# Two transformer layers on one core: an order of work of its own for the first and last windows of each layer, and an earlier load of the second causal window

## The chip, the cores and the metric

One core of one Trainium2 chip runs the whole program in one launch. The metric is the time of one execution on the device in microseconds; the number compared is the median of several executions. A change below 0.2% of it is not told apart from none here.

## The reference, cut to what matters

The input `x` is (4, 1024, 128) in float32. Four residual steps follow one another, each on the layer norm of `x`:

```python
x = x + attn_a(layernorm(x))     # 16 heads of 8, softmax over all 1024 keys
x = x + ffn(layernorm(x))        # silu(x Wg^T) * (x Wu^T), then Wd^T; hidden 384
x = x + attn_b(layernorm(x))     # the same attention with a causal mask
x = x + ffn(layernorm(x))
```

In the attention `q, k, v` come from one projection with bias, the scores are divided by sqrt(8), and an output projection with bias follows.

## The kernel before

Layer 0 is the attention over all keys, layer 1 the causal one. Each has 16 windows: 4 sequences by 4 groups of 4 heads (named a to d here). A window has two halves of 512 queries (f = 0, 1). Its work is of five kinds:

- A **job** (L1110, TensorE) computes 128 queries by up to 512 keys of plain scores into one PSUM bank, and VectorE takes their row maxima (L888, or L884 with the mask on the diagonal). Layer 0 has 64 jobs for a window, layer 1 has 36. Jobs go round a ring of banks: 3 to 6 in layer 0, 4 to 6 in layer 1.
- A **shift** unit: when the jobs of a half are done, GpSimd splits the negated maxima in two parts, TensorE transposes them (L1162), ScalarE copies them to `shift_rows` (L672), and SyncE sends them by DMA into two rows of the query operand (L433). The scores of that half wait for the DMA.
- A **scores** unit (L1144, in layer 1 with mask products L1152): 128 keys by 512 queries with the shift, for one head (single) or two (double-width), into one or two banks; ScalarE takes the exponential out of PSUM into `probs` (L656). A step is the four heads of one key block. Layer 0 uses single units in a ring of banks 0 to 2, and in its last window from step 5 on double-width units in banks 0-1 and 2-3. Layer 1 uses double-width units in the same two pairs throughout.
- The **sums** of a step (L1178): the four heads' probabilities by the values, into bank 7; after a half ScalarE copies the bank out (L663).
- A **norm** unit: TensorE transposes those sums (L1036), ScalarE copies them to `att_raw` (L677), VectorE inverts the denominators (L919), GpSimd multiplies (L549).

Every engine walks the same list, `Plan.walk`, in order. It is written out by hand as one string of letters for a window: j a job, s a scores unit, p sums, h and H the shift of half 0 and 1, N and n the norm of half 0 and 1. In the kernel before, that one string is repeated for all windows, with jobs some 48 (layer 0) or 37 (layer 1) ahead of the scores; at the ends of a layer letters that fall outside are dropped. A scores, shift or norm unit may start on TensorE when the unit that last had its banks has been copied out (`units_before`); the first double-width unit of layer 0 waits for all units before it and for all jobs.

While the last window's scores are still running, each layer starts on chunk 0 of the output projection and the feed-forward (`early_chunk`, at the steps `project_at`): ScalarE gathers heads (L686), TensorE transposes (L1036), ScalarE copies (`copy_ot`, L693), TensorE projects (`project`, L1194, bank 6), VectorE adds and normalises, TensorE transposes (`transpose_ffn_xn`), ScalarE copies (`copy_ffn_xt`, L700) and VectorE takes the remainder (`split_ffn_xt`, L943); then the same gather and transposes for chunk 1. Banks 4 and 5 hold these transposes.

Between the layers the feed-forward of layer 0 and the projections of layer 1 run chunk by chunk. SyncE stores each chunk's query and key parts to DRAM (`store_parts`, after L628 on ScalarE and L816 on VectorE) and loads a window's operands from there (`load_operands`, 14 DMAs, 1 MB); three operand buffers go round. Window 0 of layer 1 is loaded after the second chunk is stored, window 1 only after the last. Both belong to sequence 0, that is to the first two chunks. Some 18 (TensorE) or 22 (VectorE) jobs of layer 1 already run in this stage.

Of the kernel before, what the change touches and what calls it, by code (L numbers as in the profile page):

```python
# [14 lines left out]
B, S, E, H = 4, 1024, 128, 16  # L15
# [16 lines left out]
WINDOWS = B * GROUPS  # L32
# [12 lines left out]
BUFS = 3  # L45
PROBS = 6
PROB_STEPS = PROBS // 2
SEM_DMA = 16


class Plan:
# [9 lines left out]

    def __init__(self, causal, heads, unit_ring, job_ring, alternate, order, jobs_ahead, sums_behind, project_at, wide_step=99, tiles=None):
# [4 lines left out]
        self.paired = range(0 if causal else jobs_ahead)  # L69
# [9 lines left out]
        stream = []  # L79
# [20 lines left out]
        ends = {"H": ("shift", 0, 1), "h": ("shift", 1, 0), "N": ("norm", 0, 0), "n": ("norm", -1, 1)}  # L100

        self.walk = []
        jobs = taken = 0
        last_unit = {}
        for turn in range(-2, WINDOWS + 1):
            j, u, k = jobs_ahead, 0, -sums_behind
            for letter in order:
                if letter == "j":
                    w, x = turn + j // len(stream), stream[j % len(stream)]
                    j += 1  # L110
                    if 0 <= w < WINDOWS:
                        self.walk.append(("job", w, jobs, x))
                        jobs += 1
                elif letter == "s":
                    w, x = turn, units[u]
                    u += 1
                    if w == WINDOWS - 1 and x[0] >= wide_step:
                        if x[1][0] % 2 == 1:
                            continue
                        x = x[0], (x[1][0], x[1][0] + 1)  # L120
                        self.wide_from = min(self.wide_from, taken)
                    if 0 <= w < WINDOWS:
                        self.walk.append(("scores", w, taken, x))
                        last_unit[w, x[0]] = taken
                        taken += 1
                elif letter == "p":
                    w, x = turn + k // n, k % n
                    k += 1
                    if 0 <= w < WINDOWS:
                        self.walk.append(("sums", w, last_unit[w, x], x))  # L130
                else:
                    kind, dw, f = ends[letter]
                    if 0 <= turn + dw < WINDOWS:
                        self.walk.append((kind, turn + dw, taken, f))
                        taken += 1
        assert all(item[0] != "job" for item in self.walk[[i for i, item in enumerate(self.walk) if item[0] == "scores"
                                                           and item[2] >= self.wide_from][0]:]) if wide_step < n else True
# [12 lines left out]

    def ends_half(self, job):
# [2 lines left out]

PAIR_UNITS, HEAD_UNITS = ((0, 1), (2, 3)), ((0,), (1,), (2,), (3,))
PLANS = [Plan(causal=False, heads=HEAD_UNITS, unit_ring=3, job_ring=4, alternate=True,
              order="sjjsjpsjjjsspsjjsjspsjjsjspsjsjsjjsjssjjsjspHssjjsjpsjjsjspjjsjsspjsjssjsjjsnjsjjsspjssjsjpjssjsjpjssjsjpsjjsjspsjjsjspsjjsjsjsjsjsNhjjsjsspssjjjsps",
              jobs_ahead=48, sums_behind=2, project_at=(9, 11, 14), wide_step=5),
         Plan(causal=True, heads=PAIR_UNITS, unit_ring=2, job_ring=3, alternate=True,
              order="jsjjsjHpjssjjsspjjjssppjsjsjpjjssjpjjsjspjjsjspjjsjspjjjhnNjsjjspjjsjspjjssp",  # L160
              jobs_ahead=37, sums_behind=1, project_at=(4, 6, 10),
              tiles=("230 130 330 000+020 200+220 110+310 010+210 300+320 030 100+120",
                     "231 200 101+121 031 220 301+321 000 310 201+221 331 110 001+021 300 230 131 010 130 030 120 320 011+211 100 020 111+311 210 330"))]
# [7 lines left out]
def transformer_pair_kernel(nc, x_in, wqkv_a, bqkv_a, wout_a, bout_a, wqkv_b, bqkv_b, wout_b, bout_b,  # L171
# [10 lines left out]
    with ExitStack() as ctx:  # L182
# [171 lines left out]
        def _(sp):  # L354
# [46 lines left out]
            for layer, plan in enumerate(PLANS):  # L401
# [183 lines left out]
        def _(act):  # L585
# [56 lines left out]
            for layer, plan in enumerate(PLANS):  # L642
# [59 lines left out]
                def early_chunk(i):  # L702

                    if i == plan.project_at[0] - 1:
                        act.wait_ge(att_ready, half_base + 2 * GROUPS + 2)
                        gather_heads(0, 0)
                    if i == plan.project_at[0]:
                        copy_ot(0, 4)
                    if i == plan.project_at[2]:
                        copy_ffn_xt(0, 4)  # L710
                        gather_heads(1, 1)
                        copy_ot(1, 5)

                def take_weights(k):
                    act.wait_ge(setup_psum, 2 + k)
# [57 lines left out]
        def _(dve):  # L773
# [140 lines left out]
            for layer, plan in enumerate(PLANS):  # L914
# [30 lines left out]
                def early_chunk(i):  # L945

                    if i == plan.project_at[1]:
                        dve.wait_ge(x_biased, layer + 1)
                        add_projection(0)
                        projected_moments(0)  # L950
                        normalise_rows(0)
                    if i == plan.project_at[2]:
                        split_ffn_xt(0, 4)
# [59 lines left out]
        def _(pe):  # L1013
# [105 lines left out]
            for layer, plan in enumerate(PLANS):  # L1119
# [81 lines left out]
                def early_chunk(i):  # L1201

                    if i == plan.project_at[0]:
                        pe.wait_ge(ring_free, job_base + plan.jobs_all)
                        transpose_ot(0, 4)
# [123 lines left out]
```

## Time and profile before

| | |
|---|---|
| Median of 3 runs | 1323.11 us (1322.62 to 1324.69) |
| The profiled execution | 1321.39 us, of which its span 1319.5 us |
| Busy: TensorE, VectorE, ScalarE | 96%, 88%, 76% of the span |
| Layer 0's last job to its last exponential | 670.45 to 705.22 us |
| Layer 1's window 0, first scores to the next window's first | 832.40 to 863.42 us |

Times in the views count from the start of the span. PE is TensorE, DVE VectorE, ACT ScalarE, POOL GpSimd, SP SyncE. A row of a timeline gives start, length, engine, line, operation, what it writes and reads, how many in a row, and in brackets the engine's idle time before it and what ended it. In a row of a stretch each engine has its busy time and the number of its instructions; then come the granted clock of TensorE (1.00 is 2.4 GHz, 0.50 is 1.2 GHz), the busy share of the DMA engines and GB/s.

### The profile page before, as it was taken

The page shows a single profiled execution, that of the slowest core. Times are in us where ns is not written, and L with a number is a line of the kernel's source. Part 1 is how long each engine was busy: PE and PEld are TensorE (multiplying, and loading weights), DVE is VectorE, ACT ScalarE, POOL GpSimd, SP SyncE. Part 2 cuts the span into 40 slices and gives each one's busy share as a digit, 9 for nine tenths or more (in the row PEclk, how much of TensorE's full clock was granted, in tenths as well). Part 3 has the DMA queues.
Part 4 walks back from the last instruction along what each step waited for, and adds up shares of the span by engine and source line. Part 5 has one row for each costly group of instructions (what it writes and reads, how often), then busy time and mean ns, then how long its engine had stood idle before and what let it go on. Part 6 is the DMA issues. An engine that isn't in the chain of part 4 may idle for free.

```text
span 1319.5 us, 26665 instructions
## 1 busy us (share of the span) xinstructions
PE 1270.7 (96%) x9681; PEld 648.6 (49%) x9681; DVE 1162.8 (88%) x2979; ACT 1002.3 (76%) x1791; POOL 142.6 (11%) x309
## 2 busy tenths in 40 slices
PE   8899999999999999999997998899999999999898
PEld 6444343434343434343434875455555555555487
DVE  7689999999999999999934988699999999999376
ACT  8678888888888888888885552477877777777743
POOL 5630000000000000000001210200000000000011
PEclk9689999999999999999998997699999999999999
DMA  7611011111011111001000242212211221130001
GB/s 212 206 33 34 16 20 34 34 34 34 18 17 34 34 33 34 22 14 34 2 2 0 81 128 86 60 35 51 51 35 34 55 47 35 37 64 2 3 25 40
DMA packets 40059, 58.43 MB, mean 44 GB/s; under 512 B 7796, under 2 KB 19448, under 8 KB 39928
## 3 DMA queue, kind: packets, MB, share of 16 engines
q1 hardware_dynamic: 39928, 56.72, 18.0%
q8 instruction: 77, 1.26, 0.4%
q14 instruction: 54, 0.44, 0.1%
HBM read 36.77 MB, written 18.87 MB: 42 GB/s over the span
## 4 chain that ended last, share of the span: by engine, by line
PE 88%; DVE 5%; ACT 3%; issue 2%; DMA 1%; POOL 1%; SPq 0%; DVEq 0%; POOLq 0%
PE psum L1178 30%; PE psum L1110 21%; PE psum L1144 20%; PE psum L1265 4%; PE psum L1036 3%; PE psum L1249 2%; PE psum L1152 2%; ACT probs L656 2%; DVE maxima L888 1%; PE psum L1047 1%; DVE hid L966 1%; PE psum L1194 1%; PE psum L1085 1%; PE psum L1021 1%; PE psum L1162 1%
## 5 line engine op out<-in xcount | busy, mean ns | idle before, releaser
L656 ACT ACTIVATE probs<-psum 128x512 f32<-128x512 f32 (+3 forms) x1386 | 822.1, 669 | 174.2 <-PE psum L1144 89.5
L888 DVE TENSOR_REDUCE maxima<-psum 128x1 f32<-128x512 f32 x1232 | 767.8, 680 | 27.0 <-PE psum L1110 23.9
L1144 PE MATMUL psum<-qop,kop 64*128 64x512 f32 (+3 forms) x1792 | 513.7, 422 | 9.1 <-ACT probs L656 7.5
L1110 PE MATMUL psum<-kop,qop 62*128 62x512 f32 (+2 forms) x1744 | 499.7, 426 | 9.8 <-DMA kop<-k_parts 5.5
L1178 PE MATMUL psum<-probs,v 128*32 128x512 f32 (+3 forms) x3584 | 436.6, 563 | 1.1 <-ACT sums L663 1.1
L1144 PEld LDWEIGHTS psum<-qop,kop 64*128 64x128 f32 x1792 | 255.4, 188 | 213.4 <-ACT probs L656 186.2
L1110 PEld LDWEIGHTS psum<-kop,qop 62*128 62x128 f32 x1744 | 252.4, 189 | 214.8 <-DVE maxima L884 93.7
L884 DVE CUSTOM_DVE_ANT_0 junk<-psum,mask 128x384 bf16<-128x384 f32 (+3 forms) x512 | 222.3, 485 | 20.5 <-PE psum L1110 20.1
L1178 PEld LDWEIGHTS psum<-probs,v 128*32 128x32 f32 x3584 | 72.4, 109 | 112.8 <-issue 83.4
L1152 PE MATMUL psum<-half_ident,key_mask 64*128 64x64 bf16 x1024 | 83.2, 197 | 0.0
L539 POOL TENSOR_TENSOR shift<-negmax,zeros 128x16 bf16<-128x16 f32 x64 | 14.1, 220 | 567.6 <-DVE negmax L896 557.4
L549 POOL TENSOR_TENSOR att<-att_raw,rden 128x128 f32<-128x128 f32 x64 | 26.1, 407 | 423.8 <-DVE rden L919 423.8
L1249 PE MATMUL psum<-ffn_xt,gate_up_w 128*128 128x512 f32 x192 | 52.6, 409 | 6.0 <-DVE hid L966 5.9
L796 DVE TENSOR_TENSOR x<-psum,x 128x512 f32<-128x512 f32 x32 | 22.1, 689 | 38.6 <-PE psum L1194 24.9
L1152 PEld LDWEIGHTS psum<-half_ident,key_mask 64*128 64x128 bf16 x1024 | 45.3, 96 | 19.7 <-issue 8.2
L1265 PE MATMUL psum<-down_w,hid 128*128 128x128 f32 x384 | 49.0, 285 | 4.7 <-DVE hid L966 4.7
L748 ACT ACTIVATE hid<-psum 128x512 f32<-128x512 f32 x48 | 28.4, 597 | 30.3 <-PE psum L1249 30.0
L1265 PEld LDWEIGHTS psum<-down_w,hid 128*128 128x128 f32 x384 | 46.1, 198 | 7.8 <-DVE hid L966 7.2
L623 ACT ACTIVATE qk<-psum,bqk 128x512 f32<-128x512 f32 x32 | 21.1, 682 | 36.2 <-PE psum L1047 36.1
L884 DVE DVE_READ_ACCUMULATOR2_ANT maxima<- 128x1 f32 x512 | 42.4, 83 | 0.0
L1036 PE MATMUL psum<-ident,sums 128*128 128x128 f32 x256 | 38.7, 283 | 2.3 <-ACT sums L663 1.6
L1249 PEld LDWEIGHTS psum<-ffn_xt,gate_up_w 128*128 128x128 f32 x192 | 33.7, 189 | 14.7 <-DVE hid L966 8.4
(102 smaller groups left out, 732.2 us busy)
## 6 DMA issues: line engine op xcount, KB each, us to landing
qop<-q_parts SPq DMA_DIRECT2D x256, 64.0 KB
kop<-k_parts SPq DMA_DIRECT2D x64, 128.0 KB
kop<-k_parts SPq DMA_DIRECT2D x128, 64.0 KB
q_parts<-parts SPq DMA_DIRECT2D x24, 256.0 KB, 2.9
k_parts<-parts SPq DMA_DIRECT2D x24, 256.0 KB, 3.0
x<-in_L_attn_a_x SPq DMA_DIRECT2D x8, 256.0 KB, 4.2
q_parts<-att SPq DMA_DIRECT2D x8, 256.0 KB, 3.6
k_parts<-att SPq DMA_DIRECT2D x8, 256.0 KB, 3.8
```

The source lines that it names most:

```text
L549: nc.gpsimd.tensor_tensor(dst, att_raw[:, f, :, :, 0:HD], rden[:, f].rearrange("p t (h o) -> p t h o", o=1).broadcast_to([P, TPC, HG, HD]) ...
L656: nc.scalar.activation(probs[:, slot, heads[0] % 2:heads[-1] % 2 + 1, c0:], psum[:, bank:bank + len(heads), c0:], ACT.Exp, scale=SCORE_SCA ...
L748: nc.scalar.activation(hid[:, c, :], psum[:, 2 + 2 * (c % 2), :], ACT.Silu, scale=DEQUANT).then_inc(silu_ready, 1)
L884: ins = nc.vector.tensor_tensor_reduce(out=junk[:, slot, column:column + width], in0=src, in1=mask[:, CHUNK - width:], scale=1.0, scalar=L ...
L888: ins = nc.vector.tensor_reduce(dst, src, AX_X, ALU.max)
L1036: ins = nc.tensor.transpose(psum[:, bank, t * P:(t + 1) * P], src[:, t, :], ident[:])
L1110: ins = mm(psum[:, bank, column:column + width], qop[rows, buf, f, r, qb * P:(qb + 1) * P].bitcast(F32R), kop[rows, buf, r, kh * CHUNK:kh ...
L1144: ins = mm(psum[:, bank + k, c0:], kop[rows, buf, c // 2, j * P:(j + 1) * P].bitcast(F32R), qop[rows, buf, f, c // 2, c0:].bitcast(F32R), ...
L1152: ins = mm(psum[:, bank + k, at:at + TILE_ROWS], key_mask[rows, part, :], half_ident[rows], start=False, stop=part == 1)
L1178: ins = mm(psum[32 * c:32 * c + 32, 7, c0:], v[:, at:at + 32], probs[:, slot, c % 2, c0:], start=(j == 0), stop=(s == plan.half_end[f]), t ...
L1249: ins = mm(psum[:, 2 + 2 * (c % 2) + k, :], gate_up_w[:, k, c, :].bitcast(F32R), ffn_xt[:, part].bitcast(F32R), start=part == 0, stop=part ...
L1265: ins = mm(psum[:, 7, t * P:(t + 1) * P], hid[:, c, t * P:(t + 1) * P], down_w[:, c, :], start=(c == 0), stop=(c == FB - 1))
```

## The change

Each layer gets three strings: `opening` and `closing` are walked once, `order` (unchanged) 14 times between them. In layer 0 the opening gives the same list as before. In its closing, half 1's shift comes behind step 5 in place of three heads into step 4, double-width units begin at step 4 in place of 5, they go round three pairs of banks (0 to 5) in place of two, and the norms of window 14's half 1 and window 15's half 0 stand behind the last scores. As banks 4 and 5 are taken, `early_chunk` uses bank 6 for all transposes of layer 0, and TensorE waits for VectorE's `split_ffn_xt` ahead of the second `transpose_ot`. In layer 1 the opening has 32 jobs ahead of the first scores in place of 38, shift 0 stands behind 26 jobs in place of 29, the jobs of window 1 are spread among the scores, and the opening meets the old list at its place 110; in the closing shift 1 of the last window comes behind one more scores unit, norm 1 of window 14 comes earlier (ahead of step 4) and norm 0 of window 15 at the very end. SyncE loads window 1 of layer 1 straight behind window 0.

```diff
+WIDE_RING = 3
...
+        for letter in opening + order * (WINDOWS - 2) + closing:
...
     def bank(self, unit):
         if unit >= self.wide_from:
-            return (unit - self.wide_from) % 2 * 2
+            return (unit - self.wide_from) % WIDE_RING * 2
...
         if unit >= self.wide_from:
-            return unit - (unit > self.wide_from)
+            return unit - min(unit - self.wide_from, WIDE_RING - 1)
...
(layer 0)
+              closing="ssjpsjjsjspjsjjsspjjssjspsjjssjjssjjSSpSSpHSSpSSpSSpSpSSSpSpSSpSSpSSpSSpSnppNn",
-              jobs_ahead=48, sums_behind=2, project_at=(9, 11, 14), wide_step=5),
+              jobs_paired=48, project_at=(9, 11, 14)),
(layer 1)
+              opening="jjjjjjjjjjjjjjjjjjjjjjjjjjhjjjjjjsjjsjsjsjjpjjHsjsjspjjspjssjjpjsjsjpjsjjNhjssjjpjjssjjpjsjjpjjsjsjpjjsjspjjsjsjjsp",
               order="jsjjsjHpjssjjsspjjjssppjsjsjpjjssjpjjsjspjjsjspjjsjspjjjhnNjsjjspjjsjspjjssp",
-              jobs_ahead=37, sums_behind=1, project_at=(4, 6, 10),
+              closing="ssspHssspsspnssppsspsspsspsspsspsspssppNn",
+              jobs_paired=0, project_at=(4, 6, 10),
...
+CHUNK_BANKS = (6, 6, 6, 6), (4, 6, 4, 5)
...
                 load_operands(0, 0)
+                if layer == 1:
+                    load_operands(1, 1)
                 store_parts(layer, 1, 1)
...
                     sp.wait_ge(query_rows, 2)
-                load_operands(1, 1)
+                    load_operands(1, 1)
...
-                        copy_ot(0, 4)
+                        copy_ot(0, CHUNK_BANKS[layer][0])
...
                     if i == plan.project_at[2]:
-                        transpose_ffn_xn(0, 4)
-                        transpose_ot(1, 5)
+                        transpose_ffn_xn(0, CHUNK_BANKS[layer][2])
+                        if layer == 0:
+                            pe.wait_ge(ffn_low_ready, 1)
+                        transpose_ot(1, CHUNK_BANKS[layer][3])
```

The last window's end of layer 0 in the list before was:

```
...sjsjsjjssssspHsSpSSpSpSSSnSpSSpSpSSpSpSSpSSSNSpSSpppn
```

## Rows read from the trace of the kernel before

**Rows 1.** The page, part 1: busy time of each engine.

```profile
PE 1270.7 (96%) x9681; PEld 648.6 (49%) x9681; DVE 1162.8 (88%) x2979; ACT 1002.3 (76%) x1791; POOL 142.6 (11%) x309
```

**Rows 2.** Busy time by stretch, layer 0's close; columns named by engine.

```profile
690.00:700.00 10.00, 7.34 (x41) 3.15 (x40) 4.01 (x15) 7.42 (x10) 1.68 (x3) 0.82 0.00 0
...
670.45:705.22 34.77, 29.27 (x180) 10.52 (x179) 4.45 (x17) 26.86 (x36) 2.53 (x6) 0.90 0.01 1
```

**Rows 3.** Timeline of ScalarE, layer 0's close; in brackets the idle time before.

```profile
667.90 4.03 ACT L656 ACTIVATE probs<-psum 128x512 f32<-128x512 f32 x8 [0.32 <-PE psum L1144]
...
673.69 1.02 ACT L656 ACTIVATE probs<-psum 128x1024 f32<-128x1024 f32 x1 [0.60 <-PE psum L1144]
...
691.76 4.69 ACT L656 ACTIVATE probs<-psum 128x1024 f32<-128x1024 f32 x5 [1.32 <-PE psum L1144]
...
698.38 0.58 ACT L700 CAST ffn_xt<-psum 128x512 fp32r<-128x512 f32 x1
...
698.86 0.62 ACT L686 COPY ot<-att 128x512 f32<-128x512 f32 x1
...
700.68 0.58 ACT L693 COPY ot_t<-psum 128x512 f32<-128x512 f32 x1 [1.20 <-PE psum L1036]
...
703.28 1.94 ACT L656 ACTIVATE probs<-psum 128x1024 f32<-128x1024 f32 x2 [2.01 <-PE psum L1144]
```

**Rows 4.** Timeline of VectorE, layer 0's close.

```profile
656.84 13.58 DVE L888 TENSOR_REDUCE maxima<-psum 128x1 f32<-128x512 f32 x22
...
698.99 0.69 DVE L943 TENSOR_TENSOR ffn_xt<-psum,ffn_xt 128x512 fp32r<-128x512 f32 x1 [2.09 <-ACT ffn_xt L700]
```

**Rows 5.** Timeline of TensorE, layer 0's close.

```profile
674.58 0.73 PE L1144 MATMUL psum<-qop,kop 64*128 64x512 f32 x4
...
675.24 1.07 PE L1178 MATMUL psum<-probs,v 128*32 128x512 f32 x8
...
699.53 1.11 PE L1036 MATMUL psum<-ident,ot 128*128 128x128 f32 x4 [1.19 <-ACT ot L686]
```

**Rows 6.** Timeline of SyncE, layer 1's opening: DMA issues.

```profile
822.29 1.71 SPq L396 DMA_DIRECT2D qop<-q_parts  x4
...
828.14 9.35 SPq L433 DMA_DIRECT2D qop<-shift_rows  x4
```

**Rows 7.** Timeline of TensorE, layer 1's opening.

```profile
831.84 0.79 PE L1110 MATMUL psum<-kop,qop 62*128 62x512 f32 x2 [5.54 <-DMA kop<-k_parts]
...
832.40 0.66 PE L1144 MATMUL psum<-qop,kop 64*128 64x512 f32 x2
...
844.28 1.21 PE L1144 MATMUL psum<-qop,kop 64*128 64x512 f32 x2
```

**Rows 8.** Timeline of VectorE, layer 1's opening.

```profile
832.79 0.69 DVE L884 CUSTOM_DVE_ANT_0 junk<-psum,mask 128x512 bf16<-128x512 f32 x1 [5.46 <-PE psum L1110]
...
863.76 0.18 DVE L896 TENSOR_REDUCE negmax<-maxima 128x16 f32<-128x32 f32 x1
```

**Rows 9.** Busy time by stretch, layer 1's opening.

```profile
820.00:823.00 3.00, 3.00 (x9) 1.70 (x8) 2.97 (x7) 0.83 (x2) 0.00 (x0) 0.50 0.54 164
...
832.40:844.28 11.88, 11.88 (x92) 7.36 (x88) 7.81 (x36) 5.57 (x9) 9.73 (x5) 0.50 0.36 76
...
844.28:863.76 19.48, 19.38 (x172) 9.71 (x168) 16.96 (x48) 14.09 (x19) 0.00 (x0) 0.94 0.07 11
```

**Rows 10.** Chain that ended last, two transfers in it: start, length, what.

```profile
63.74 1.96 DMA qop<-shift_rows
...
819.23 3.00 DMA k_parts<-parts
```

**Rows 11.** Timeline of ScalarE, feed-forward stage between the layers.

```profile
787.35 1.05 ACT L628 CAST parts<-qk 128x1024 fp32r<-128x1024 f32 x1
```

**Rows 12.** Timeline of ScalarE, layer 1's close.

```profile
1246.21 0.28 ACT L677 COPY att_raw<-psum 128x144 f32<-128x144 f32 x1 [0.41 <-PE psum L1036]
...
1247.10 1.51 ACT L656 ACTIVATE probs<-psum 128x768 f32<-128x768 f32 x2 [0.18 <-PE psum L1152]
```

More of the change, by code:

```diff
@@ L47, with __init__ @@
 PROB_STEPS = PROBS // 2
+WIDE_RING = 3
 SEM_DMA = 16
 class Plan:
-    def __init__(self, causal, heads, unit_ring, job_ring, alternate, order, jobs_ahead, sums_behind, project_at, wide_step=99, tiles=None):
+    def __init__(self, causal, heads, unit_ring, job_ring, alternate, opening, order, closing, jobs_paired, project_at, tiles=None):
         self.causal, self.heads, self.unit_ring, self.job_ring = causal, heads, unit_ring, job_ring
@@ L68, in __init__ @@
         self.job_bank = 7 - job_ring
-        self.paired = range(0 if causal else jobs_ahead)
+        self.paired = range(jobs_paired)
         self.steps = []
@@ L99, in __init__ @@
         assert order.count("j") == len(stream) and order.count("s") == len(units) and order.count("p") == n
-        ends = {"H": ("shift", 0, 1), "h": ("shift", 1, 0), "N": ("norm", 0, 0), "n": ("norm", -1, 1)}
+        ends = {"H": ("shift", 1), "h": ("shift", 0), "N": ("norm", 0), "n": ("norm", 1)}
         self.walk = []
-        jobs = taken = 0
+        jobs = taken = units_begun = sums_begun = 0
+        ends_begun = dict.fromkeys(ends, 0)
         last_unit = {}
[L105 to L135, printed above, removed]
@@ new lines, in __init__ @@
+        for letter in opening + order * (WINDOWS - 2) + closing:
+            if letter == "j":
+                if jobs < WINDOWS * len(stream):
+                    self.walk.append(("job", jobs // len(stream), jobs, stream[jobs % len(stream)]))
+                    jobs += 1
+            elif letter in "sS":
+                w, x = units_begun // len(units), units[units_begun % len(units)]
+                if letter == "S":
+                    x = x[0], (x[1][0], x[1][0] + 1)
+                    self.wide_from = min(self.wide_from, taken)
+                assert letter == "S" or taken < self.wide_from
+                units_begun += 1 + (letter == "S")
+                self.walk.append(("scores", w, taken, x))
+                last_unit[w, x[0]] = taken
+                taken += 1
+            elif letter == "p":
+                w, x = divmod(sums_begun, n)
+                self.walk.append(("sums", w, last_unit[w, x], x))
+                sums_begun += 1
+            else:
+                kind, f = ends[letter]
+                self.walk.append((kind, ends_begun[letter], taken, f))
+                ends_begun[letter] += 1
+                taken += 1
@@ L136, in __init__ @@
+        assert jobs == WINDOWS * len(stream) and units_begun == WINDOWS * len(units) and sums_begun == WINDOWS * n
+        assert all(count == WINDOWS for count in ends_begun.values())
         assert all(item[0] != "job" for item in self.walk[[i for i, item in enumerate(self.walk) if item[0] == "scores"
-                                                           and item[2] >= self.wide_from][0]:]) if wide_step < n else True
+                                                           and item[2] >= self.wide_from][0]:]) if closing.count("S") else True
@@ L156 @@
 PLANS = [Plan(causal=False, heads=HEAD_UNITS, unit_ring=3, job_ring=4, alternate=True,
+              opening="jjjjjjjjjjjjjjjjjjjjjjjjjjjjjjjjjjjjjjjjjjhjjjjjjsjjsjsjjjsssjjsjspsjjsjspsjsjsjjsjssjjsjspHssjjsjpsjjsjspjjsjsspjsjssjsjjsjsjjsspjssjsjpjssjsjpjssjsjpsjjsjspsjjsjspsjjsjsjsjsjsNhjjsjsspssjjjsps",
               order="sjjsjpsjjjsspsjjsjspsjjsjspsjsjsjjsjssjjsjspHssjjsjpsjjsjspjjsjsspjsjssjsjjsnjsjjsspjssjsjpjssjsjpjssjsjpsjjsjspsjjsjspsjjsjsjsjsjsNhjjsjsspssjjjsps",
-              jobs_ahead=48, sums_behind=2, project_at=(9, 11, 14), wide_step=5),
+              closing="ssjpsjjsjspjsjjsspjjssjspsjjssjjssjjSSpSSpHSSpSSpSSpSpSSSpSpSSpSSpSSpSSpSnppNn",
+              jobs_paired=48, project_at=(9, 11, 14)),
          Plan(causal=True, heads=PAIR_UNITS, unit_ring=2, job_ring=3, alternate=True,
+              opening="jjjjjjjjjjjjjjjjjjjjjjjjjjhjjjjjjsjjsjsjsjjpjjHsjsjspjjspjssjjpjsjsjpjsjjNhjssjjpjjssjjpjsjjpjjsjsjpjjsjspjsjjsp",
               order="jsjjsjHpjssjjsspjjjssppjsjsjpjjssjpjjsjspjjsjspjjsjspjjjhnNjsjjspjjsjspjjssp",
-              jobs_ahead=37, sums_behind=1, project_at=(4, 6, 10),
+              closing="ssspHssspsspnssppsspsspsspsspsspsspssppNn",
+              jobs_paired=0, project_at=(4, 6, 10),
               tiles=("230 130 330 000+020 200+220 110+310 010+210 300+320 030 100+120",
                      "231 200 101+121 031 220 301+321 000 310 201+221 331 110 001+021 300 230 131 010 130 030 120 320 011+211 100 020 111+311 210 330"))]
+CHUNK_BANKS = (6, 6, 6, 6), (4, 6, 4, 5)
 SHIFT_PAIR = 2 * -(-[item[0] for item in PLANS[0].walk].index("shift") // 4)
@@ L707, in early_chunk @@
                     if i == plan.project_at[0]:
-                        copy_ot(0, 4)
+                        copy_ot(0, CHUNK_BANKS[layer][0])
                     if i == plan.project_at[2]:
-                        copy_ffn_xt(0, 4)
+                        copy_ffn_xt(0, CHUNK_BANKS[layer][2])
                         gather_heads(1, 1)
-                        copy_ot(1, 5)
+                        copy_ot(1, CHUNK_BANKS[layer][3])
                 def take_weights(k):
@@ L952, in early_chunk @@
                     if i == plan.project_at[2]:
-                        split_ffn_xt(0, 4)
+                        split_ffn_xt(0, CHUNK_BANKS[layer][2])
                 for kind, w, number, what in plan.walk[layer * DVE_JOBS_AHEAD:]:
@@ L1204, in early_chunk @@
                         pe.wait_ge(ring_free, job_base + plan.jobs_all)
-                        transpose_ot(0, 4)
+                        transpose_ot(0, CHUNK_BANKS[layer][0])
                     if i == plan.project_at[1]:
```

## The prediction, on record before the run

> **What bounds the kernel now.** I read the page first: TensorE is busy nearly all the time, VectorE and ScalarE much of it [rows 1]. That is an average over stages, and the change leaves the 14 middle windows of both layers as they are. So I read only the three seams: in each, which engine's idle time moves the end, and what it waits for.
>
> At the close of layer 0 VectorE works without a pause until its last job, 670.42 us [rows 4]; by then ScalarE has taken five of a row of eight exponentials that began at 667.90 [rows 3]. From there to the last exponential, 703.28 + 1.94 = 705.22, only ScalarE's work is long: 26.86 us busy in 34.77 [rows 2]. It idles 7.9 us, always for scores that TensorE has not yet issued: 0.60 at the first double-width unit, 1.32 behind the projection, 1.20 and 2.01 around the transposes of chunk 1 [rows 3]. The seam is bound by ScalarE with holes, and the holes come from having two bank pairs.
>
> At the opening of layer 1 VectorE's job stream sets the pace. It stops for 5.46 us because TensorE waits 5.54 us for window 1's keys [rows 7, 8]. SyncE begins that load at 822.29 and is done issuing at 828.14; the shift of window 0, long ready, is issued behind it [rows 6]. The first scores start at 832.40 [rows 7]. From there to the end of window 1's maxima at 863.76 [rows 8] TensorE is busy throughout, first at 0.50 of its clock, then at 0.94; VectorE is busy 7.81 of 11.88 us, then 16.96 of 19.48 [rows 9].
>
> At the close of layer 1 the two norms cost ScalarE a small hole: about 0.41 us of idle time, two copies and 0.18 [rows 12].
>
> **Close of layer 0.** The 16 single units and all jobs now come ahead of the first double-width unit. VectorE is saturated before it, so its last job still ends at about 670.5. The first double-width unit waits for that job and for all exponentials before it; with the 0.60 us that its predecessor waited for its two products [rows 3], ScalarE starts at about 671.1. Then the sum over ScalarE:
>
> - Work: the 26.86 us of before; four singles (about 0.50 each, 4.03 for 8) become two double-width ones (4.69 for five, so 0.92 each): minus 0.2. Two norm copies leave this stretch: minus 0.6. Makes 26.1.
> - Can TensorE feed it? A step needs four products (0.66 to the next operation) and the sums (1.00), 1.66 us [rows 5], against 1.84 for two exponentials. With a third pair it may be two units ahead, so the projection (1.1) fits in the lead. I count nothing there and 0.3 for what I overlook.
> - The chunk 1 transposes stay a hole, and the new wait sits in it. TensorE can't transpose until ScalarE has gathered (698.86 + 0.62) and now until VectorE has subtracted (0.69, begun when the copy at 698.38 ends) [rows 3, 4]; both end within 0.2 us of each other, 699.5 and 699.7. What is queued behind that wait on TensorE: the transposes, window 15's last two score units and three sums, and ScalarE waits for these. Transposes at full rate about 0.6 (1.11 at half [rows 5]), so the hole is about 1.0, and 0.5 more before the last unit, as sums stand between the two. Before, the two holes were 1.20 + 2.01.
> - The deferred norms run on TensorE while ScalarE is at its last exponential and at the copy of the last sums; I count nothing. If that cover were gone, each costs a set of transposes and a copy, about 0.9.
>
> Total 26.1 + 0.6 + 0.3 + 1.5 = 28.5 us from 670.45, against 34.77: a gain of 6.3. Before, the granted clock fell here (0.82 in 690 to 700 [rows 2]); the hole at the transposes may make it fall again, which would stretch the last units by some 2 us at most (these products and sums doubled). I take 6.0, bounds 4 and 8.
>
> **Opening of layer 1, the load.** SyncE issues 14 DMAs more behind window 0's, which before took it from 822.29 to 828.14, 5.9 us [rows 6], in the feed-forward stage. Queued behind them are the stores of chunk 3. ScalarE needs that buffer again two chunks later, at 787.35 [rows 11]; the chunk's stores were due at about 766, so at 772 now. A landing of 3.0 us as at the seam [rows 10] leaves some 10 us. I count nothing. Without that cover it costs up to the 5.9.
>
> **Opening of layer 1, the order.** With the queue free, the shift of window 0 waits only until SyncE has seen the last store land, 819.23 + 3.00 = 822.2 [rows 10]. One issue (0.43 for each of four before [rows 6]) and 1.96 for the second with its landing [rows 10]: the first scores can start at about 825.0 in place of 832.4. VectorE runs dry for about 1 us there, as only 32 jobs stand ahead.
>
> From there 4 jobs more than before lie between the first scores and step 4, and 2 more up to the end of window 1's jobs. TensorE was already at half clock before the DMA wait (0.50 in 820 to 823, while busy 3.00 of 3.00 [rows 9]), so I take the first part again at half clock: the 11.88 us of before plus 4 jobs at 0.4 (0.79 for two [rows 7]) is 13.5, step 4 at about 838.5. The second part took 19.48 with VectorE busy 16.96; two jobs more are 1.2 us of VectorE, of which its idle time takes some: 20.3. Window 1's maxima end at about 858.8 in place of 863.76: a gain of 5.0.
>
> Bounds: above, VectorE without a pause from where it stopped, 832.79 - 5.46 = 827.33, with its 24.8 us of work [rows 8, 9], ends at 852.1, gain 11.7; with the 1 us that it runs dry and another 0.7 of small pauses, 10. Below, half clock for all of window 0 is a rival of its own. From the repeated order on the list is the old one, so the shift in time stays.
>
> By the Trainium skill, page "TensorE: Matmul & The Clock Gate", section "Loop structure matters more than you think", a long wait for a DMA between matmuls makes TensorE go cold, and dense matmuls keep it at full rate; the wait goes, so by that page the opening would run at full rate, and its gain would be the 10 just named in place of 5. The rows bear out only half of it: the clock was at 0.50 before the wait began, and stayed there for 11.88 us of full busy time after it.
>
> **Close of layer 1.** Without norms at step 9 the hole of 0.41 + 0.18 and a copy of 0.28 go [rows 12]: 0.9. Norm 1 of window 14 now stands ahead of step 4 and costs a copy there, about 0.3. The later shift has a few units until it is needed and costs nothing by the 1.96 of [rows 10]. Gain 0.6, bounds minus 0.5 and 1.5.
>
> **Sum.** 6.0 + 5.0 + 0.6 = 11.6 us. The profiled execution took 1321.4, so 1309.8; the median of the runs shown is 1.7 above it, so 1311.5.
>
> **The rivals.**
>
> - *The clock comes back with the first scores.* For it: no 5.5 us gap any more. Against it: half clock under full load in [rows 9]. VectorE then sets the pace of the opening, which gives the 10 worked out above, 5 more than forecast: 1306.5. Chance 0.22.
> - *The wait in the opening is only exchanged.* The early scores and sums hold TensorE at half clock, the jobs behind them come late, and VectorE's hole moves from one place to several. The opening gives 0 to 1, total 1316. For it: VectorE idled 4 of 11.88 us there with TensorE busy throughout [rows 9]. Chance 0.14.
> - *The third pair does nothing,* because bank 6 in common and the new wait hold TensorE up as the two pairs did. 1317.5. Against it: the two waits end 0.2 us apart. Chance 0.05.
> - *Slower.* Place: window 0 of layer 1. If the thinner mix of scores and jobs keeps the clock at 0.50 all through, the 19.48 us of the second part double (it was at 0.94), costing 18.2: total 1311.5 + 18.2 = 1329.7. Half clock takes back half of its length, so this side begins when it lasts 23 us beyond step 4, to about 862. For it: 0.50 through 11.88 us of full load; against it: it did come back before. Chance 0.04.
>
> The forecast itself, 1308 to 1315, has 0.55. The range from 1305 to 1317 takes in the first two rivals and leaves out about 0.15. A measurement here tells about 0.2% (2.6 us) from no change: faster than that 0.92, within 0.04, slower 0.04.
>
> **What the profile would show.** Close of layer 0: ScalarE idle 2 to 3 us in place of 7.9 between the last job and the last exponential, double-width exponentials 0.92 apart, one hole at the transposes. Layer 1: no wait for `k_parts` at the 37th job, first scores some 7 us sooner against the end of the last store, clock 0.50 for a dozen us after it, ScalarE at 787 (moved by the first gain) not waiting for a store. Close: no hole at step 9. Wrong it would be if VectorE's last job of layer 0 came late, if the shift's transfer were still late, or if the clock stayed low.

## The result and the profile after

The changed kernel took 1312.93 us (median of 6 runs, 1310.55 to 1314.25), the one before 1322.86 beside it (6 runs, 1320.22 to 1324.69): a ratio of 0.9923, 95% interval 0.991 to 0.9937. Forecast were 1311.5 us and a range of 1305 to 1317. The medians differ by 9.9 us. The profiled execution took 1313.18 us with a span of 1311.3, 8.2 less than the span before.

To see where these 8.2 us come from, I cut both spans at the same five instructions: ScalarE's copy of `att_raw` ahead of layer 0's close, the start of its copy of layer 0's last sums, its cast for the stores of chunk 3 [rows 11], SyncE's issue of the last of these stores, and the copy of the shift that ends the opening of layer 1.

| Stage, us | before | after | difference |
|---|---|---|---|
| start to `att_raw` (655.92, 655.33) | 655.92 | 655.33 | -0.59 |
| layer 0's close, to the last sums (706.40, 701.13) | 50.48 | 45.80 | -4.68 |
| between the layers, to the cast (787.35, 783.46) | 80.95 | 82.33 | +1.38 |
| to the last store's issue (819.23, 816.84) | 31.88 | 33.38 | +1.50 |
| layer 1's opening, to the shift copy (866.08, 858.63) | 46.85 | 41.79 | -5.06 |
| the rest of layer 1, its close in it | 453.42 | 452.67 | -0.75 |

The change doesn't touch the code of the first, third and fourth stage, apart from the early load, which is issued in the third. In the last row, the repeated windows took 353.97 us in both (866.08 to 1220.05, 858.63 to 1212.60).

**Layer 0's close.** First VectorE, then ScalarE, then TensorE, in the timelines after:

```profile
661.43 9.37 DVE L892 TENSOR_REDUCE maxima<-psum 128x1 f32<-128x512 f32 x15 [0.73 <-PE psum L1114]
```

```profile
665.43 4.21 ACT L660 ACTIVATE probs<-psum 128x512 f32<-128x512 f32 x8 [0.47 <-PE psum L1148]
671.49 1.94 ACT L660 ACTIVATE probs<-psum 128x1024 f32<-128x1024 f32 x2 [1.84 <-PE psum L1148]
674.39 1.94 ACT L660 ACTIVATE probs<-psum 128x1024 f32<-128x1024 f32 x2 [0.96 <-PE psum L1148]
...
685.26 9.59 ACT L660 ACTIVATE probs<-psum 128x1024 f32<-128x1024 f32 x10
...
696.80 0.59 ACT L697 COPY ot_t<-psum 128x512 f32<-128x512 f32 x1 [0.97 <-PE psum L1040]
...
698.67 1.02 ACT L660 ACTIVATE probs<-psum 128x1024 f32<-128x1024 f32 x1 [0.35 <-PE psum L1148]
...
701.13 0.59 ACT L667 COPY sums<-psum 128x512 f32<-128x512 f32 x1 [1.27 <-PE psum L1182]
```

```profile
670.95 0.81 PE L1148 MATMUL psum<-qop,kop 64*128 64x512 f32 x4 [1.99 <-DVE maxima L892]
671.69 1.94 PE L1182 MATMUL psum<-probs,v 128*32 128x512 f32 x8
...
696.10 0.66 PE L1040 MATMUL psum<-ident,ot 128*128 128x128 f32 x4 [2.09 <-DVE ffn_xt L947]
...
697.12 1.06 PE L1182 MATMUL psum<-probs,v 128*32 128x512 f32 x8
```

Ten double-width exponentials stand in a row, 0.96 us apart; before, five at most did. The hole of 1.32 us [rows 3] is gone, and those of 1.20 and 2.01 are down to 0.97 and 0.35. New are 1.84 and 0.96 us at the first double-width units: ScalarE is through with its single units before VectorE is with its jobs, TensorE stands still for 1.99 us, and its clock falls behind that (busy times by stretch; the third figure from the end is the granted clock):

```profile
668.00:671.00 3.00, 1.01 (x6) 0.45 (x5) 2.97 (x6) 1.65 (x4) 0.00 (x0) 1.00 0.00 0
671.00:674.00 3.00, 3.00 (x14) 0.90 (x16) 0.03 (x1) 1.94 (x2) 0.44 (x2) 0.58 0.00 0
...
670.80:699.69 28.89, 26.57 (x177) 9.05 (x177) 3.94 (x16) 25.72 (x32) 1.72 (x4) 0.94 0.01 2
```

The sums at 671.69 took 1.94 us, against 1.07 at full rate [rows 5]. A second wait of TensorE, 2.09 us ahead of 696.10, had no such effect: the sums behind it took 1.06 us.

**Between the layers.** TensorE waits 3.12 us for VectorE, as long as before; in this profile the clock is at half level behind the wait, in that of before it was not:

```profile
709.43 2.08 PE L1255 MATMUL psum<-ffn_xt,gate_up_w 128*128 128x512 f32 x4 [3.12 <-DVE hid L970]
```

```profile
706.00:709.00 3.00, 0.32 (x3) 0.07 (x1) 1.53 (x8) 1.11 (x3) 1.26 (x2) 1.00 0.00 0
709.00:712.00 3.00, 2.57 (x8) 2.18 (x9) 1.36 (x3) 0.60 (x1) 0.00 (x0) 0.50 0.00 0
```

**Layer 1's opening.** SyncE issues the shift 3.02 us behind the last store, with no load in front of it; 2.70 us later the first scores start. VectorE, out of jobs, waits 1.67 us in place of 5.46 [rows 8]:

```profile
819.86 1.36 SPq L437 DMA_DIRECT2D qop<-shift_rows  x2
```

```profile
822.56 0.80 PE L1148 MATMUL psum<-qop,kop 64*128 64x512 f32 x2 [1.16 <-DMA qop<-shift_rows]
```

```profile
824.11 0.69 DVE L892 TENSOR_REDUCE maxima<-psum 128x1 f32<-128x512 f32 x1 [1.67 <-PE psum L1114]
...
856.53 0.18 DVE L900 TENSOR_REDUCE negmax<-maxima 128x16 f32<-128x32 f32 x1
```

```profile
822.56:834.98 12.42, 12.42 (x93) 7.03 (x93) 8.16 (x33) 5.78 (x9) 6.89 (x3) 0.50 0.13 35
...
834.00:837.00 3.00, 3.00 (x21) 1.36 (x20) 1.90 (x11) 1.58 (x2) 3.00 (x1) 0.50 0.73 159
837.00:840.00 3.00, 3.00 (x21) 1.18 (x24) 2.32 (x11) 2.44 (x4) 0.84 (x3) 0.71 0.57 122
```

TensorE is busy without a break from the first scores at 822.56 to the end of these stretches, and until about 838.7 at 1.2 GHz (worked out from the 0.71 of the last one).

### The profile page after: what moved, and what is told of

Its sections match the earlier page's. It is cut to its first block, busy times and chain, and to the rows that moved or that the text cites. A ratio compares the mean times of both kernels' runs of the same rounds, so it can differ in the third digit from the quotient of the medians.

```text
span 1311.3 us, 26664 instructions
## 1 busy us (share of the span) xinstructions
PE 1269.7 (97%) x9681; PEld 647.3 (49%) x9681; DVE 1163.2 (89%) x2979; ACT 1002.3 (76%) x1789; POOL 143.0 (11%) x309
## 4 chain that ended last, share of the span: by engine, by line
PE 88%; DVE 5%; ACT 3%; issue 2%; DMA 1%; SPq 1%; POOL 0%; DVEq 0%; POOLq 0%; ACTq 0%
PE psum L1182 30%; PE psum L1114 22%; PE psum L1148 20%; PE psum L1271 4%; PE psum L1040 3%; PE psum L1255 3%; PE psum L1156 2%; ACT probs L660 2%; DVE maxima L892 1%; PE psum L1051 1%; DVE hid L970 1%; PE psum L1198 1%; PE psum L1089 1%; PE psum L1025 1%; PE psum L1166 1%
## 5 line engine op out<-in xcount | busy, mean ns | idle before, releaser
L543 POOL TENSOR_TENSOR shift<-negmax,zeros 128x16 bf16<-128x16 f32 x64 | 14.2, 222 | 559.5 <-DVE negmax L900 548.1
L553 POOL TENSOR_TENSOR att<-att_raw,rden 128x128 f32<-128x128 f32 x64 | 26.1, 408 | 420.8 <-DVE rden L923 420.8
L752 ACT ACTIVATE hid<-psum 128x512 f32<-128x512 f32 x48 | 28.5, 598 | 30.8 <-PE psum L1255 30.4
L1040 PE MATMUL psum<-ident,sums 128*128 128x128 f32 x256 | 38.9, 283 | 0.6 <-ACT sums L667 0.4
```

The source lines that it names most:

```text
L553: nc.gpsimd.tensor_tensor(dst, att_raw[:, f, :, :, 0:HD], rden[:, f].rearrange("p t (h o) -> p t h o", o=1).broadcast_to([P, TPC, HG, HD]) ...
L752: nc.scalar.activation(hid[:, c, :], psum[:, 2 + 2 * (c % 2), :], ACT.Silu, scale=DEQUANT).then_inc(silu_ready, 1)
L1040: ins = nc.tensor.transpose(psum[:, bank, t * P:(t + 1) * P], src[:, t, :], ident[:])
```

## The experiments

The theory: layer 0's close, the load and the opening list each do what the prediction says. Against it stand: one of the parts does all of it, and the 2.9 us lost between the layers (third and fourth stage) are a price of the change or chance. The stages of all profiles, cut as above, in us:

| Profile | close | between | to the store | opening |
|---|---|---|---|---|
| before | 50.48 | 80.95 | 31.88 | 46.85 |
| the change | 45.80 | 82.33 | 33.38 | 41.79 |
| new close of layer 0 alone | 45.77 | 82.37 | 33.40 | 45.44 |
| load alone | 50.46 | 83.65 | 31.17 | 41.41 |
| load and opening list | 50.42 | 80.96 | 33.42 | 41.94 |
| opening list alone | 50.34 | 80.95 | 33.44 | 49.30 |
| close with two pairs | 49.34 | 82.44 | 33.44 | 45.37 |
| old list, three pairs | 49.01 | 82.54 | 33.43 | 48.46 |
| close with four more singles | 43.59 | 83.70 | 31.16 | 48.42 |
| change, opening filled | 45.70 | 82.45 | 34.19 | 38.30 |
| change, old opening list | 45.71 | 82.42 | 33.43 | 41.36 |
| change, hole between filled | 45.85 | 80.96 | 31.14 | 41.84 |
| change, singles, opening filled | 43.54 | 80.94 | 34.25 | 38.49 |
| all three | 43.55 | 80.95 | 32.63 | 38.90 |

The stages between the layers hold the same instructions in nearly all of them, and yet take 80.95, 82.4 or 83.7 us, and 31.2 to 33.4: in these stages the clock falls in some profiles and not in others, and each kernel has one profile. The opening, too, scatters where the load comes late: with the same code in it as before it took 45.4 us twice, 46.9 and 48.5 twice, with the clock back some 7.7 us behind the first scores in the first two and 14.2 in the others; what else they differ by lies ahead of the first scores. With the early load and no fillers in it or just ahead of it, it took 41.4 to 41.9 in all five profiles.

### One part alone: close, load, opening list

The diffs are against the changed kernel, if not said otherwise.

```diff
 # new close of layer 0 alone: layer 1's lists and its load as before
-                if layer == 1:
-                    load_operands(1, 1)
 # load alone: all three lists, the two pairs of banks, CHUNK_BANKS[0] and TensorE's waits as before
-WIDE_RING = 3
+WIDE_RING = 2
 # load and opening list: as the last, with layer 1's new opening
 # opening list alone: as the last, without the early load
```

Expected of the close alone: 

> Only the new closing of layer 0 with its three pairs of banks; load, opening and closing of layer 1 as before. Theory (each seam is a term of its own): the last exponential of layer 0 comes about 5 us sooner (4.9 in the changed kernel), ScalarE idles about 4 us between the last job and it, nothing else moves: 1.318 ms or 0.996 of the time before. On the stretch between the layers: if the half clock seen there in the changed kernel (1.6 us lost from the last exponential to chunk 3) is caused by the new closing, it shows here again and the total gain is about 3.5 us; if it is chance, that stretch takes the 59.9 us of before. Rival (the third pair does nothing, the seams hang together): less than 2 us.

Measured: 1317.93 us (10 runs), ratio 0.9969, interval 0.9955 to 0.9983, beside 1322.17 us of the kernel before.

Expected of the load alone: 

> Only the early load of window 1, all orders as before. Theory: VectorE no longer stops at the 37th job, the first scores wait only for the shift's transfer and 38 jobs and come about 4.5 us sooner; gain 4 to 5 us, so the order adds next to nothing. Rival (the early first scores make the gain): the 38 jobs still stand ahead and ScalarE's work begins hardly sooner; gain under 2 us.

Measured: 1315.3 us (4 runs), ratio 0.9942, interval 0.992 to 0.9965.

Expected of load and list: 

> The early load and the new opening of layer 1, both closings as before. Theory: 5.0 us from the first store to window 1's first scores, as in the changed kernel; gain 5 us. Rival (the stretch between the layers loses 1.5 us to the early load's place in the queue): that stretch takes 58.6 in place of 57.1 us here as well, gain 3.5.

Measured: 1317.19 us (5 runs), ratio 0.9946, interval 0.9925 to 0.9967.

Expected of the list alone: 

> Only the new opening of layer 1, the load of window 1 still behind the last store. Theory: the shift is issued behind that load as before, the first scores start some 1 to 2 us sooner at most, jobs of window 1 wait for their keys behind the first scores; gain 0 to 2 us. Rival (the order alone makes the gain): 4 to 5 us.

Measured: 1326.25 us (10 runs), ratio 1.0033, interval 1.0023 to 1.0043. Slower, which neither the theory nor its rival had said. Its profile is 4.5 us longer than that of before: 2.45 us of that are in the opening, 1.56 in the stage to the last store, and 1.49 in the rest of layer 1, where the clock fell in this profile alone (0.67 in 1255 to 1260); the stages ahead of these took 1.0 us less.

So the early load does the whole of the opening's gain: 3.4 to 7.1 us, depending on which two profiles are compared. The first scores of the three, on TensorE (load alone; load and list; list alone):

```profile
827.94 1.12 PE L1148 MATMUL psum<-qop,kop 64*128 64x512 f32 x2
```

```profile
825.98 0.80 PE L1148 MATMUL psum<-qop,kop 64*128 64x512 f32 x2 [1.18 <-DMA qop<-shift_rows]
```

```profile
833.38 0.79 PE L1146 MATMUL psum<-qop,kop 64*128 64x512 f32 x2 [9.02 <-DMA qop<-shift_rows]
```

With the load, the new list starts the scores 1.9 us sooner after nearly the same last store (issued at 820.28 and 820.23), and the opening is 0.5 us longer all the same. TensorE is busy from there on, and the clock comes back at about 842 with either list (first the load alone, then load and list):

```profile
840.00:843.00 3.00, 3.00 (x18) 1.39 (x20) 2.13 (x7) 1.96 (x3) 0.00 (x0) 0.60 0.32 51
```

```profile
840.00:843.00 3.00, 3.00 (x19) 1.13 (x16) 1.92 (x10) 2.32 (x4) 1.26 (x3) 0.60 0.64 130
```

So a job moved behind the first scores is only done later. Without the load, the list leaves TensorE 9.02 us without work, as fewer jobs stand ahead of the wait, in place of the 5.54 of before [rows 7].

### The whole change with layer 1's old opening

```diff
-              opening="jjjjjjjjjjjjjjjjjjjjjjjjjjhjjjjjjsjjsjs...
+              opening="jjjjjjjjjjjjjjjjjjjjjjjjjjjjjhjjjjjjjjjsjjsjH...
```

Expected: 

> The whole change, but with layer 1's old opening list. The early load alone took all of the opening's gain above (from the last store's issue to the first steady window's shift copy 41.4 us with the old list, 41.8 and 41.9 us with the new one), so: within 1 us of the whole change, 1312 to 1314 us. The prediction's rival reading, that the new list starts the scores earlier and is worth some 2 us beside the load: about 1315 us.

Measured: 1313.11 us (1308.51 to 1314.03, 4 runs), ratio 0.9922, interval 0.9897 to 0.9948, as the whole change; the opening took 41.36 us, against 41.79. No gain of the list shows beside the load.

### Layer 0's close: the third pair, the list, and its start

```diff
 # against the new close alone: two pairs
-WIDE_RING = 3
+WIDE_RING = 2
 # old list, three pairs
-              closing="ssjpsjjsjspjsjjsspjjssjspsjjssjjssjjSSpSSpHSS...
+              closing="sjjsjpsjjjsspsjjsjspsjjsjspsjsjsjjssssspHsSpSS...
 # new close alone, four more singles
-...jjssjjSSpSSpH...
+...jjssjjsssspSSpH...
-            return (unit - self.wide_from) % WIDE_RING * 2
+            return (unit - self.wide_from + 2) % WIDE_RING * 2
-            return unit - min(unit - self.wide_from, WIDE_RING - 1)
+            return unit - min((unit - self.wide_from) or 2, WIDE_RING - 1)
```

Expected of the list with two pairs: 

> Layer 0's new closing list alone (first layer's list, no early load, old lists of layer 1), but with two pairs of banks in turn instead of three. If the third pair is what closes the gaps between the wide exponentials, they come back: some 24 wide ones at about 0.4 us for every second one and the holes of 0.7 to 2.0 us of the list before, some 3 to 5 us, so about 1321 to 1322 us, as before the change. If the new order of the list does it (single heads until VectorE's last job is near, sums put between), the gain of 4.2 us stays: about 1318 us.

Measured: 1322.55 us (10 runs), ratio 1.0008, interval 0.9996 to 1.0019: no gain is left.

Expected of the third pair with the old list: 

> The other half: layer 0's old closing list, with three pairs of banks in turn. If the third pair does it: about 1318 to 1319 us, and the gaps of 0.2 to 0.7 us between the wide exponentials are gone. If the list does it: about 1322 us, with the gaps of 1.2 and 2.0 us near the end (they stand behind the sums of the list) as before.

Measured: 1321.9 us (10 runs), ratio 0.9989, interval 0.9977 to 1.0001: none that can be told from the noise.

Either half alone shortens the close by 1.1 and 1.5 us, both together by 4.7. With two pairs the new list has its holes back (ScalarE; 1.51 us at the last unit), and with three pairs the old list keeps the hole that its own order makes:

```profile
703.13 1.02 ACT L658 ACTIVATE probs<-psum 128x1024 f32<-128x1024 f32 x1 [1.51 <-PE psum L1146]
```

```profile
701.57 1.94 ACT L658 ACTIVATE probs<-psum 128x1024 f32<-128x1024 f32 x2 [1.28 <-PE psum L1146]
...
705.67 0.58 ACT L665 COPY sums<-psum 128x512 f32<-128x512 f32 x1 [2.16 <-PE psum L1180]
```

In both, and before (0.82 [rows 2]), the clock is down at the end of the close; in the change it isn't, as the sums at 697.12 show. So part of the 4.7 us is likely the clock; how much is not separated. The same stretch, two pairs and then the old list:

```profile
700.00:703.00 3.00, 3.00 (x13) 0.68 (x12) 0.00 (x0) 1.51 (x2) 0.00 (x0) 0.58 0.00 0
```

```profile
700.00:703.00 3.00, 3.00 (x20) 0.90 (x16) 0.00 (x0) 1.72 (x3) 0.00 (x0) 0.57 0.00 0
```

Expected of four more singles: 

> Layer 0's new closing alone, with the four heads of step 4 as single heads behind the last jobs, and the first wide unit in banks 4 and 5, which no single head uses. If the 1.84 and 0.96 us in which ScalarE waited at 671 to 675 us are VectorE's last job plus the two banks that the single heads hold, the four single exponentials (4 x 0.53 us) cover them: about 2.3 us less than the new closing alone, 1315.6 us. If the stall only moves behind the four heads, or TensorE's half clock there is what costs: 1317.5 to 1318 us, as the new closing alone.

Measured: 1316.15 us (4 runs), ratio 0.9955, interval 0.9938 to 0.9971, against 0.9969 for the new close alone. The intervals overlap; the stage shows it: 43.59 us in place of 45.77, and 43.54 and 43.55 in the two further kernels with these singles, against 45.70 to 45.85 in the five with the new close and without them. ScalarE and the clock where TensorE had waited:

```profile
665.39 6.18 ACT L658 ACTIVATE probs<-psum 128x512 f32<-128x512 f32 x12 [0.47 <-PE psum L1146]
672.12 1.94 ACT L658 ACTIVATE probs<-psum 128x1024 f32<-128x1024 f32 x2 [0.55 <-PE psum L1146]
...
674.09 5.77 ACT L658 ACTIVATE probs<-psum 128x1024 f32<-128x1024 f32 x6
```

```profile
671.00:674.00 3.00, 2.77 (x23) 0.74 (x15) 0.00 (x0) 2.45 (x5) 0.44 (x2) 1.00 0.01 3
```

The hole of 1.84 us is down to 0.55, and the 0.96 behind it is gone, as is the half clock.

### Matmuls that compute nothing, in TensorE's waits

`keep_busy(count, bank)` issues so many products of `ident` with itself, 128x128 by 128x128, into a bank that nothing else holds just then. The rows show each of them as two.

```diff
+                if layer == 0:
+                    keep_busy(4, 0)          # bank 0, behind the last stage between the layers
                 pe.wait_ge(x_new, (layer + 1) * CHUNKS)
...
+                        if layer == 1 and number == 1:
+                            keep_busy(6, 7)  # bank 7, ahead of the first causal scores
...
                         transpose_ot(turned, 0)
+                    if layer == 0 and ffn == 0:
+                        keep_busy(10, 7)     # the second kernel has this one alone
```

Expected of the filled opening: 

> The whole change, with 4 and 6 matmuls of 128x128 by 128x128 into free banks, ahead of the jobs behind the residual of the last chunk and ahead of the first causal scores (they compute nothing that is used). If TensorE's short waits there (0.2 to 1.2 us each from 812 to 822 us) hold its clock at half level through the opening, the clock comes back some 10 us earlier than 838 us, and the opening, in which TensorE is busy all the time, loses 3 to 6 us: 1307 to 1310 us. If the clock doesn't answer to them, they cost their own 1 to 2 us or nothing: 1312.5 to 1315 us.

Measured: 1310.34 us (1309.07 to 1311.6, 4 runs), ratio 0.991, interval 0.9895 to 0.9925, which overlaps with the change's; the stage shows the gain. The opening fell from 41.8 to 38.3 us (38.5 and 38.9 in the two further kernels with these fillers). Six filling matmuls and the clock behind them:

```profile
822.88 2.93 PE L1025 MATMUL psum<-ident 128*128 128x128 f32 x12
825.73 0.65 PE L1148 MATMUL psum<-qop,kop 64*128 64x512 f32 x2
```

```profile
824.00:827.00 3.00, 3.00 (x25) 2.41 (x24) 0.20 (x1) 0.50 (x1) 0.00 (x0) 0.65 0.02 5
827.00:830.00 3.00, 2.62 (x30) 1.16 (x24) 2.98 (x8) 2.10 (x4) 0.00 (x0) 1.00 0.00 0
```

They put off the first scores to 4.20 us behind the shift's issue, from 2.70, and with the four ahead of them the stage before took 0.8 us more; but the clock is back at 2.4 GHz at about 826 (worked out from the 0.65), not at 838.7. So half clock was the bound of the opening, and VectorE comes next: busy 2.98 of 3.00.

Expected of the filled hole between the layers: 

> The whole change, with 10 matmuls of 128x128 by 128x128 into a free bank in the 3.12 us hole of TensorE ahead of the last third of the first gate and up products of layer 0 (about 2.5 us at full clock; nothing uses them). If that hole is what takes the clock to half level right behind layer 0's close (1.6 us lost there in the profile of the change, and 2.1 to 2.7 us in others), the clock stays at full level to 790 us and the time falls by 1 to 2.5 us: 1310.5 to 1312 us. If the clock falls there for another reason, no change or the fillers' overhang: 1313 to 1314 us.

Measured: 1309.58 us (1308.46 to 1313.24, 4 runs), ratio 0.9912, interval 0.9891 to 0.9933, which overlaps with the change's. In its profile the clock stays at full level and the stage takes 80.96 us:

```profile
705.14 2.40 PE L1025 MATMUL psum<-ident 128*128 128x128 f32 x20
708.42 1.20 PE L1255 MATMUL psum<-ffn_xt,gate_up_w 128*128 128x512 f32 x4 [0.89 <-DVE hid L970]
```

### Together

Expected of the singles with the filled opening: 

> The whole change with both of the mends that helped alone: the four heads of step 4 as single heads with the first wide unit in banks 4 and 5 (1.8 us less than the new closing alone), and the 10 filling matmuls in front of and in the opening (2.6 us less than the whole change). If they stand in different stages and add: 1308.5 us. If one takes from the other (the clock's state at the end of the first layer carries over): 1310 to 1311 us.

Measured: 1307.02 us (1305.55 to 1309.59, 4 runs), ratio 0.989, interval 0.9871 to 0.9909: below the change's 0.991 to 0.9937. The two gains add: the close took 43.54, the opening 38.49. Its diff is that of the four singles and that of the filled opening; the next kernel has the filled hole as well.

Expected of all three mends: 

> The whole change with the singles, the filled opening and the filled hole between the layers together. In the profile of the singles with the filled opening the clock was at full level from 703 to 780 us without the fillers between the layers, in others it was not: where it falls it costs 1.6 to 2.7 us. If the fillers hold it there in every execution and take nothing from the rest: about 1305.5 us, with a narrower spread of the runs. If the executions without them mostly have the full clock there already, or the fillers only move the fall to the next hole: 1307 us, as without them.

Measured: 1308.34 us (1307.26 to 1308.72, 4 runs), beside 1323.58 of the kernel before; ratio 0.9887, interval 0.9871 to 0.9904. The same as without the fillers between the layers: there the profile shows 80.94 us without and 80.95 with them. These two have the lowest medians of this study.

## Why the prediction was right, and where it wasn't

**Close of layer 0, from the last job.** The sum gave 28.5 us; from the last job's end (670.80) to the last exponential's (699.69) it took 28.89. By terms: ScalarE's work 26.1, measured 25.72; its start behind the last job 0.6, measured 0.69; the holes at the transposes 1.0 and 0.5, measured 0.97 and 0.35; 0.3 for what was overlooked, measured 0.96, the sums at half clock. The third pair feeds ScalarE as said, but only with the new list; that the holes come from having two pairs was a part of the cause. The rival that the third pair does nothing fell with the whole, though it comes close for the old list, where the pair took 1.5 us off the stage. A deferred norm, counted at nothing, has its transposes ahead of the last sums: the copy of these sums begins 1.44 us behind the last exponential, before 1.18. The difference takes the 4.94 us gained up to the last exponential down to the table's 4.68; that the transposes cause it is likely, but not tested.

**Close of layer 0, VectorE's last job.** This step failed. "VectorE is saturated before it, so its last job still ends at about 670.5": from the same `att_raw` copy it ended after 15.47 us (655.33 to 670.80), before after 14.53 (655.92 to 670.45), as the new list starves VectorE once for 0.73 us. That takes 0.94 off the 6.0 us. And the prediction took no account of TensorE being idle while it waits for that job: 1.99 us, behind which the clock fell. Four single units there, with the first double-width unit in banks that the wait doesn't concern, took 2.2 us off the stage.

**The opening.** Forecast 5.0, measured 5.06; that they meet so closely is luck in two ways. The terms: first scores 2.8 us behind the landing of the last store, measured 2.70 behind the shift's issue, which waits for that landing; from there to the end of window 1's maxima 13.5 + 20.3 = 33.8, measured 12.42 + 21.55 = 33.97 (822.56 to 834.98 to 856.53). The first part was put too long and the second too short: by the two lists three more jobs lie in each, not four and two, and half clock went on to 838.7, into the second part. And the sum starts from the one profile of before, whose 46.85 us lie in the middle of the 45.4 to 48.5 that this opening takes. The cause was wrong in part: I gave the load and the order a common sum, and the order has no share in it. "VectorE's job stream sets the pace" was wrong too: it is TensorE at half clock, as the fillers show.

The first rival, that the clock comes back with the first scores, did not happen by itself: the clock was at 0.50 for some 16 us of matmuls without a break. By the Trainium skill, page "TensorE: Matmul & The Clock Gate", section "Loop structure matters more than you think", a long wait for a DMA between matmuls makes TensorE go cold and dense matmuls keep it at full rate. The row at 822.56 to 834.98 us speaks against taking the wait away as the cure: the wait is down to 1.16 us, and dense matmuls went on at half clock. That the long wait made the clock fall no row here shows: it was at 0.50 before the wait of 5.54 us began [rows 7, 9]. With six 128x128 matmuls ahead of the scores, and four ahead of the last store, the clock did come back, and the opening gained 3.5 us where the rival had put 5. Whether it was their kind or the filling of the wait that did it is not separated, nor whether the four had a share.

The second rival, that the wait is only exchanged, had its mechanism right in part: VectorE was busy 8.16 of 12.42 us behind the first scores, fed late by TensorE at half clock. The gain came all the same, since the first scores start 5.72 us behind the issue of the last store, before 13.17. The slower side, half clock through all of window 0, did not come: the clock was back at 838.7.

**The load.** Counted at nothing, and nothing it was: the cast of chunk 3 (783.46) waits for no store, but starts as soon as the activation before it ends (783.43).

**Close of layer 1.** Forecast 0.6, measured 0.75 in the table's last stage. No run has this close alone, but the stage took 452.7 to 452.8 us in all six profiles with it, and 453.4 to 453.6 in seven of the eight without (454.9 in that of the list alone).

**What no term had.** 2.9 us were lost between the layers in the one profile, with instructions that hadn't changed, and 0.6 gained ahead of the close; so the three seams gave 10.5 us of the 11.6 forecast, and the span 8.2. The profiles with the new close and no fillers there show 82.3 us and more in five of six (the singles with the filled opening have 80.94), those with the old list and two pairs 80.95 in three of four; the new list with two pairs and the old with three have 82.44 and 82.54. That looks like a tendency. It isn't shown, since each kernel has one profile, and filling the hole changed the time by less than can be measured. Part of it may be why the medians of close and load alone (4.2 and 6.9 us) add up to 11.1, and the whole gave 9.9; but by the intervals each of the three is uncertain by 2 to 3 us.

## What to carry to other kernels

In a seam, ask of each engine what it does while the last item of another engine's stream ends, TensorE above all: here 1.99 us of standing still were followed by some 3 us at half clock. Such a wait has no fixed price, though: one of 2.09 us later in the same close had full clock behind it. The parts of a change, here an order and an early load, are best priced one by one: the load alone had the opening's gain, and the order without it made the kernel slower. Two mends that each take away half of a hole's causes may show nothing in the kernel's time alone, as the list and the third pair. And a stage read from one profile can be off by what the clock did in that execution, here by up to 3 us.

## What the runs showed of the hardware

The spread of this kernel's runs goes with its clock: of the runs of the kernel before beside the filled opening, those with a mean granted clock of 0.972 took 1319.5 to 1321.6 us, those with 0.968 took 1325.0 and 1325.3. Equal instructions took 80.95, 82.4 or 83.7 us in one stage: behind the same wait of 3.12 us the clock stayed up (before), was down in part of 709 to 715 us (the change: 0.50, then 0.93), or in most of 706 to 715 (the close with four more singles: 0.53, 0.50, 0.83).

A few us of matmuls that nobody needs can be worth their time: 10 of them, 4.05 us of TensorE in the profile (1.12 and 2.93), saved 3.5 us of the opening, though the first scores came 1.5 us later behind the shift's issue, and 0.8 were lost ahead of it.
